# Tensor product of a graph network on one core: where TensorE reads a group's word, and where its loop body begins

## The chip, the core and the metric

One core of a Trainium2 chip runs the whole program. Its engines are TensorE (PE in the profile, its weight loads PEld, its sequencer PEq or PEldq), VectorE (DVE), ScalarE (ACT), GpSimd (POOL) and SyncE (SP, which starts DMAs). Each runs its own instruction stream, and they meet at semaphores. An engine's sequencer takes its stream in order: it handles registers, branches and waits itself and hands matmuls on to the array. The metric is the device time of one execution in microseconds.

## What is computed

Four layers of a graph network over 12,500 nodes and 400,000 edges, with a layer norm behind each. The change touches the last one, a tensor product over the edges. Cut to what matters (x are the node rows, sh1 the edge's direction, emb and edge_vec are inputs of the edge):

```
xs, xd = (x[edge_src], x[edge_dst])
s1 = concatenate([xs[:, :8], xd[:, :8]]); v1 = the other 24 columns of both as (16, 3)
w = _mlp(emb, fc1_w1, fc1_w2)                    # 10 -> 16 -> 512 weights of an edge
vdot1 = einsum('euk,ek->eu', v1, sh1) / SQRT3
s_t = a1 * (einsum('eu,euw->ew', s1, Wss) + einsum('eu,euw->ew', vdot1, Wvv))
v_t = a1 * (einsum('eu,euw->ew', s1, Wsv)[:, :, None] * sh1[:, None, :] + einsum('euk,euw->ewk', v1, Wvs))
w2 = _mlp(emb, fc2_w1, fc2_w2)                   # and the same once more on s_t, v_t: scal, gates, vecs
edge_out = concatenate([tanh(scal), vecs * tanh(gates)]) * norm
return segment_sum(edge_out, edge_dst)           # edges are sorted by edge_dst
```

## The kernel before

The edges are cut into 625 groups of 640 (5 tiles of 128). In this stage (`stage_tensor_product`) every engine runs one *turn* for each group, and a turn works on several groups at once, at different steps. SLOTS is 5 buffers, a loop body holds 15 turns (3 rounds of 5), and the body is run 41 times; the first and the last turns are written out beside it. The order within a turn is written out by hand in one function for each engine.

TensorE's turn is `pe_turn`. `there(i, j, off)` says whether the group `off` turns on exists, `at` names it. Before, it does in this order:

- `turn_words` (L2201, L2202): a wait and semaphore step, a register load of the group's word from SBUF and the arithmetic that cuts it up. The word tells the first block of own rows of the group two ahead (`first_ahead`) and how many visits that group (`n_ahead`) and the group three behind (`n`) need.
- `pe_contract` half 0 (matmuls L2537, 128 rows deep) and `pe_spread` half 1 (L2520, four matmuls on 32 rows each) of the group one behind,
- `pe_units` half 0 (L2509), `pe_turn_inputs` (transposes, L2547) of the next group, `pe_brackets` half 1 (L2495, four matmuls on 32 rows each),
- `pe_contract` half 1, `pe_turn_inputs` half 1,
- `pe_further_visits` for the group three behind: a test (L2572) whose body is jumped over where n is 1,
- `pe_return` (L2555), `pe_spread` half 0, `pe_units` half 1,
- `pe_own` (L2588 to L2592): the products with the own rows of the group two ahead, at an address made of `first_ahead`,
- `pe_brackets` half 0 of the next group: four matmuls in two pairs, each pair waiting (L2493) until VectorE has read the pair's two banks (`dve_second`, L2371),
- `pe_first_visit` (L2560), and `pe_own_further`: a test (L2599) whose body is jumped over where `n_ahead` is 1.

VectorE's turn runs, around the change: `dve_second` half 0 (L2371, a pair at a time), `dve_join` (L2347, needs `pe_own`), then as a new turn its own word, `dve_first` half 0 (L2363, a pair at a time, needs the pair of brackets), `dve_front` (L2354), `dve_first_visit` (L2425, needs `pe_first_visit`), `dve_second` half 1 (needs `pe_spread` half 1). `pe_spread` half 1 in turn needs, for each pair, `dve_first` half 0 of that pair, since both use the same banks. `pe_own` must wait for a DMA (`turned_in`) and for ScalarE's copies (`flipped`).

The loop jump of TensorE (L2732 in the profile) stands behind the 15th turn.

Of the kernel before, what the change touches and what calls it, by code (L numbers as in the profile page):

```python
# [14 lines left out]
ITERS = GROUPS // SLOTS  # L15
# [492 lines left out]
class Ranks:  # L508
# [7 lines left out]
    def at(self, i, n):  # L516
        return self.per * i + n
# [1641 lines left out]
def stage_tensor_product(nc, m, s):  # L2159
# [26 lines left out]
    def at(i, j, off):  # L2186
        return i + (j + off) // SLOTS, (j + off) % SLOTS

    def tile_of(j, k, off):
        return (k + (j + off) // SLOTS) % ROUNDS  # L2190

    def there(i, j, off):
        return not isinstance(i, int) or 0 <= SLOTS * i + j + off < GROUPS
# [13 lines left out]
    def turn_words(eng, i, j):  # L2207

        g = SLOTS * i + j
        if isinstance(i, int) and not 0 <= g < GROUPS:  # L2210
            first, n, _ = half_window_of(nc, eng, m, s, g + 2 if g < 0 else g - 3)
            return first, n, first, n
        return words_of(eng, g)
# [357 lines left out]
    def pe_further_visits(pe, i, j, n):  # L2571
        with pe.If(n > 1):  # L2572
            _, visits, further = half_window_of(nc, pe, m, s, SLOTS * i + j)
            pe.wait_ge(s["first_added"], ONE + SLOTS * i + j + 1)
            if not (isinstance(i, int) and SLOTS * i + j == GROUPS - 1):
                pe.wait_ge(s["summed_up"], ONE + SLOTS * i + j + 2)
            pe.sem_inc(s["going"], 1)
            with pe.Fori(1, visits) as k:
                pe.wait_ge(s["more_hot"], ONE + further + k)
                pe_product(sums_at(1), pieces(j), m["onehot_more"]).then_inc(s["summed"], 1)  # L2580
                pe.wait_ge(s["added"], ONE + further + k)
# [26 lines left out]

    def pe_turn(pe, i, j, k):

        if there(i, j, -3) or there(i, j, 2):
            _, n, first_ahead, n_ahead = turn_words(pe, i, j)
        if there(i, j, -1):
            pe_contract(pe, *at(i, j, -1), 0)
            pe_spread(pe, *at(i, j, -1), 1)
        if there(i, j, 0):
            pe_units(pe, i, j, 0)
        if there(i, j, 1):
            pe_turn_inputs(pe, *at(i, j, 1), 0)
        if there(i, j, 0):  # L2620
            pe_brackets(pe, i, j, 1)
        if there(i, j, -1):
            pe_contract(pe, *at(i, j, -1), 1)
        if there(i, j, 1):
            pe_turn_inputs(pe, *at(i, j, 1), 1)
        if there(i, j, -3):
            pe_further_visits(pe, *at(i, j, -3), n)
        if there(i, j, -1):
            pe_return(pe, *at(i, j, -1))
        if there(i, j, 0):  # L2630
            pe_spread(pe, i, j, 0)
            pe_units(pe, i, j, 1)
        if there(i, j, 2):
            pe_own(pe, *at(i, j, 2), tile_of(j, k, 2), first_ahead)
        if there(i, j, 1):
            pe_brackets(pe, *at(i, j, 1), 0)
        if there(i, j, -2):
            pe_first_visit(pe, *at(i, j, -2))
        if there(i, j, 2):
            pe_own_further(pe, *at(i, j, 2), n_ahead)  # L2640

    with nc.Block() as block:

        @block.sync
        def _(sp):
            sp_iteration(sp, 0, 0, False)
            for j in range(SLOTS):
                sp_group(sp, 0, j, 0, False)
            with sp.Fori(0, (ITERS - 2) // ROUNDS) as r:
                for i, k in rounds_of(r):  # L2650
                    for j in range(SLOTS):
                        sp_group(sp, i, j, k, True)
            for j in range(SLOTS):
                sp_group(sp, ITERS - 1, j, (ITERS - 1) % ROUNDS, True)
            sp_hot(sp, ITERS - 1, SLOTS - 1, True)
            sp.wait_ge(s["all_added"], ONE + 1)
            sp.dma_start(m["tmp"][HALF_P:P, :], m["acc"][0:HALF_P, NB * W:HALF_WINDOWS * W]).then_inc(s["halves_in"], 16)
            sp.dma_start(m["tmp"][0:HALF_P, W:NB * W], m["acc"][HALF_P:P, NB * W:(HALF_WINDOWS - 1) * W]).then_inc(s["halves_in"], 16)
            sp.wait_ge(s["finished"], ONE + 1)
            sp.dma_start(m["out"], m["x"][:, :]).then_inc(s["stored"], 16)  # L2660
            sp.wait_ge(s["stored"], 16)

        @block.gpsimd
        def _(pool):
            for j in range(3):
                pool_gather(pool, 0, j, 0, 0)
            for j in range(SLOTS):
                pool_turn(pool, 0, j, 0, 0)
            with pool.Fori(0, (ITERS - 2) // ROUNDS) as r:
                for i, k in rounds_of(r):  # L2670
                    for j in range(SLOTS):
                        pool_turn(pool, i, j, k, r if k else r + 1)
            for j in range(SLOTS):
                pool_turn(pool, ITERS - 1, j, (ITERS - 1) % ROUNDS, (ITERS - 1) // ROUNDS)
            for j in range(4):
                pool_pieces(pool, *at(ITERS, j, -4))

        @block.scalar
        def _(act):
            act_inputs(act, 0, 0)  # L2680
            act_turn(act, -1, SLOTS - 1)
            for j in range(SLOTS):
                act_turn(act, 0, j)
            with act.Fori(0, (ITERS - 2) // ROUNDS) as r:
                for i, _ in rounds_of(r):
                    for j in range(SLOTS):
                        act_turn(act, i, j)
            for j in range(SLOTS):
                act_turn(act, ITERS - 1, j)
            for j in range(3):  # L2690
                act_turn(act, ITERS, j)
            roots_act(nc, act, s, 1, m["root"][:, :])

        @block.vector
        def _(dve):
            nc.vector.memset(m["acc"][:, :], 0.0).then_inc(s["added_up"], 1)
            dve.wait_ge(s["added_up"], ONE + 1)
            _, n, _ = half_window_of(nc, dve, m, s, 0)
            dve_turned_further(dve, 0, 0, n)
            dve_join(dve, 0, 0)  # L2700
            dve_turn(dve, -1, SLOTS - 1, -1 % ROUNDS)
            for j in range(SLOTS):
                dve_turn(dve, 0, j, 0)
            with dve.Fori(0, (ITERS - 2) // ROUNDS) as r:
                for i, k in rounds_of(r):
                    for j in range(SLOTS):
                        dve_turn(dve, i, j, k)
            for j in range(SLOTS):
                dve_turn(dve, ITERS - 1, j, (ITERS - 1) % ROUNDS)
            for j in range(3):  # L2710
                dve_turn(dve, ITERS, j, ITERS % ROUNDS)
            _, n, further = half_window_of(nc, dve, m, s, GROUPS - 1)
            dve.wait_ge(s["first_gained"], ONE + GROUPS)
            dve.wait_ge(s["gained"], ONE + further + n - 1)
            link = Chain(dve, s["step"])
            cubed = lambda t: t[:, :].rearrange("p (b f) -> p b f", f=F)
            nc.vector.memset(m["tmp"][0:HALF_P, 0:W], 0.0).then_inc(s["all_added"], 1)
            link(nc.vector.tensor_tensor(m["x"][:, :], m["x"][:, :], m["acc"][:, 0:NB * W], ALU.add))
            dve.wait_ge(s["halves_in"], 32)
            link(nc.vector.tensor_tensor(m["x"][:, :], m["x"][:, :], m["tmp"][:, :], ALU.add))  # L2720
            layer_norm(nc, dve, link, s, 1, cubed(m["x"]), cubed(m["tmp"]), m["mean"][:, :], m["root"][:, :])
            nc.vector.nop().then_inc(s["finished"], 1)

        @block.tensor
        def _(pe):
            first, n, _ = half_window_of(nc, pe, m, s, 0)
            pe_own(pe, 0, 0, 0, first)
            pe_own_further(pe, 0, 0, n)
            pe_turn(pe, -1, SLOTS - 1, -1 % ROUNDS)
            for j in range(SLOTS):  # L2730
                pe_turn(pe, 0, j, 0)
            with pe.Fori(0, (ITERS - 2) // ROUNDS) as r:  # L2732
                for i, k in rounds_of(r):
                    for j in range(SLOTS):
                        pe_turn(pe, i, j, k)
            for j in range(SLOTS):
                pe_turn(pe, ITERS - 1, j, (ITERS - 1) % ROUNDS)
            for j in range(3):
                pe_turn(pe, ITERS, j, ITERS % ROUNDS)


def build(nc, d):
# [305 lines left out]
```

## Time and profile before

| | us |
|---|---|
| median of 3 runs | 25141.51 (25137.35 to 25158.99) |
| the profiled execution, its own time | 25140.86 |
| its span in the profile | 25139.1 |
| the tensor product's turns within it | about 18641 to 25086 |
| TensorE busy over the whole span | 59% |
| VectorE busy over the whole span | 61% |

The page's share of busy time covers all stages. The tensor product is the last quarter of the span, and there TensorE and VectorE are both close to full. All rows below are from that one execution; times in them count from the span's start.

### The profile page before, as it was taken

Reading aid. Unit: us, or ns where it says so; the run is one execution under the profiler, and the core shown is the slowest. Engines: PE = TensorE matmul, PEld = TensorE weight load, DVE = VectorE, ACT = ScalarE, POOL = GpSimd, SP = SyncE. Lnnn points to the kernel's source line nnn. Section 1 sums busy time; section 2 is a strip of 40 time slices with the busy share of each in tenths; the row PEclk is TensorE's granted clock in tenths of the full one; section 3 lists DMA queues with packets and bytes.
Section 4 is the critical chain, followed back from the end, with each engine's and each line's share of the span. In section 5 each row is a group of like instructions: output and inputs, shape, how many; then the busy total and the mean of one; then the engine's idle time right before and its main releaser. Section 6 shows DMA issues by size and latency. Waiting matters only on the chain. (4 is left out here: it accounts for less than half of the span.)

```text
span 25139.1 us, 445752 instructions
## 1 busy us (share of the span) xinstructions
PE 14765.1 (59%) x102440; PEld 8906.5 (35%) x102441; DVE 15355.5 (61%) x31597; ACT 5180.0 (21%) x13760; POOL 15775.7 (63%) x16798
## 2 busy tenths in 40 slices
PE   7555555576666669995100000000568888888888
PEld 5344444443434348892000000000523333333333
DVE  9766666656565654443111111599578888888888
ACT  4211111111111124441000000000023333333332
POOL 0377777677777764451677777776046666666665
PEclk9655555555555555555555555555579999999999
DMA  2466666633333335540211111122133333433333
GB/s 66 108 173 173 172 173 173 154 69 68 68 68 68 69 77 153 154 128 9 43 40 40 40 40 40 53 72 61 31 100 104 103 103 104 105 103 104 103 104 95
DMA packets 2469135, 2331.19 MB, mean 93 GB/s; under 512 B 1084287, under 2 KB 1990333, under 8 KB 2465922
## 3 DMA queue, kind: packets, MB, share of 16 engines
q1 hardware_dynamic: 1901630, 1900.27, 26.8%
q0 software_dynamic: 412544, 241.53, 6.6%
q10 hardware_dynamic: 153668, 172.93, 2.8%
q8 instruction: 717, 11.75, 0.2%
q14 instruction: 576, 4.72, 0.1%
HBM read 1765.30 MB, written 537.93 MB: 92 GB/s over the span
## 5 line engine op out<-in xcount | busy, mean ns | idle before, releaser
L768 POOL DMA_INDIRECT rows<-split_table,index x3125 | 2995.0, 958 | 1938.5 <-DMA index<-in_src 1007.0
L2255 POOL DMA_INDIRECT rows_x<-x_table,index x3125 | 2972.9, 951 | 1625.9 <-DMA index<-in_src 772.3
L1648 POOL DMA_INDIRECT rows_dram<-rows,place_now x3125 | 3026.2, 968 | 1487.9 <-issue 951.8
L884 POOL DMA_INDIRECT rows<-x_table,index x3125 | 3277.7, 1049 | 1021.1 <-issue 952.0
L1575 DVE TENSOR_REDUCE rows<-banks 128x108 f32<-128x324 f32 x1250 | 490.7, 434 | 3467.4 <-DMA rows_dram<-rows,place_now 3456.0
L1587 PE MATMUL banks<-row_pieces,hot_turned 128*128 x3125 | 393.7, 291 | 3604.0 <-DVE rows L1575 3542.1
L2371 DVE TENSOR_TENSOR second<-banks,h 128x768 f32<-128x768 f32 x2500 | 1944.7, 820 | 896.5 <-PE banks L2520 896.5
L2363 DVE TENSOR_TENSOR first<-banks,h 128x768 f32<-128x768 f32 x2500 | 1934.4, 815 | 155.7 <-issue 120.2
L576 PE MATMUL banks<-counts,low_turned 128*128 128x98 f32 x6250 | 1794.7, 435 | 79.3 <-ACT counts L564 49.5
L576 PEld LDWEIGHTS banks<-counts,low_turned 128*128 128x128 f32 x6250 | 1602.1, 315 | 204.1 <-issue 174.0
L2495 PE MATMUL banks<-u_turned,w_tensor 32*128 32x384 f32 (+1 forms) x10000 | 1529.6, 486 | 145.4 <-DVE second L2371 145.4
L1587 PEld LDWEIGHTS banks<-row_pieces,hot_turned 128*128 128x128 bf16 x3125 | 251.2, 134 | 3746.6 <-issue 3746.6
L976 PE MATMUL banks<-ident,rows 128*64 128x128 f32 x3125 | 734.1, 396 | 1305.4 <-DMA rows<-x_table,index 1301.2
L1065 PE MATMUL banks<-w,a 65*128 65x64 f32 x6250 | 1445.2, 418 | 90.4 <-DMA a<-a_dram 65.1
L1065 PEld LDWEIGHTS banks<-w,a 65*128 65x128 f32 x6250 | 1398.7, 332 | 172.5 <-issue 168.0
L2537 PE MATMUL banks<-second,w_second 128*32 128x384 f32 (+1 forms) x10000 | 1031.1, 482 | 495.9 <-issue 495.0
L2520 PE MATMUL banks<-units,unit_spread 32*128 32x384 f32 (+1 forms) x10000 | 1111.5, 516 | 0.3 <-DVE first L2363 0.3
L985 PE MATMUL banks<-flipped,w 64*64 64x512 f32 x1250 | 1104.5, 980 | 0.0
L2309 ACT COPY outputs<-banks 128x384 f32<-128x384 f32 x1250 | 531.4, 425 | 2711.3 <-PE banks L2537 2711.3
L1117 POOL TENSOR_TENSOR pieces<-rest,pieces 128x320 bf16<-128x320 f32 x625 | 479.8, 768 | 963.3 <-ACT pieces L1095 963.3
L947 ACT ACTIVATE lift<-banks,bias 64x640 f32<-64x640 f32 x625 | 492.6, 788 | 2808.8 <-PE banks L986 2790.3
L2509 PE MATMUL banks<-first,unit_sum 128*32 128x384 f32 (+1 forms) x10000 | 1063.5, 480 | 13.3 <-DVE first L2363 1.1
(480 smaller groups left out, 33435.6 us busy)
## 6 DMA issues: line engine op xcount, KB each, us to landing
h<-hidden_dram SPq DMA_DIRECT2D x1250, 320.0 KB
acc_moved<-dst_rows SPq DMA_DIRECT2D x625, 320.0 KB
src_row<-in_src_rows SPq DMA_DIRECT2D x625, 320.0 KB
hot_turned<-turned_dram SPq DMA_DIRECT2D x1250, 160.0 KB, 2.2
hot_dram<-onehot SPq DMA_DIRECT2D x625, 160.0 KB
turned_dram<-hot_turned SPq DMA_DIRECT2D x625, 160.0 KB
a_dram<-a ACTq DMA_DIRECT2D x625, 160.0 KB
a<-a_dram SPq DMA_DIRECT2D x625, 160.0 KB, 2.9
```

Of the source, the lines that this page charges most:

```text
L576: nc.tensor.matmul(self.look[:, wide], m["low_turned"][:, tile], m["counts"][:, wide], start=True, stop=False)
L768: nc.gpsimd.indirect_dma_start(out=m["rows"][j][:, t * SPLIT:(t + 1) * SPLIT], out_offset=None, in_=m["split_table"], in_offset=bass.Indir ...
L884: nc.gpsimd.indirect_dma_start(out=m["rows"][j][:, t * C2:t * C2 + F], out_offset=None, in_=m["x_table"], in_offset=bass.IndirectOffsetOnA ...
L985: nc.tensor.matmul(m["ps"][4][0:H, :], m["w"][0:C2, 0:H], flipped[:, 0:512], start=True, stop=True)
L1065: mm = nc.tensor.matmul(bank(j)[:, t * H:(t + 1) * H], m["a1"][j][0:W, t * P:(t + 1) * P], m["w"][0:W, 0:H], start=True, stop=True)
L1648: nc.gpsimd.indirect_dma_start(out=m["rows_dram"], out_offset=bass.IndirectOffsetOnAxis(ap=m["place_now"][j][:, t:t + 1], axis=0), in_=m[" ...
L2255: nc.gpsimd.indirect_dma_start(out=m["rows_x"][j][:, t * F:(t + 1) * F], out_offset=None, in_=m["x_table"], in_offset=bass.IndirectOffsetO ...
L2363: nc.vector.tensor_tensor(m["first"][2 * half + pair][:, :].rearrange("p (k e) -> p k e", k=2), bank_pair(4 + 2 * pair, width), rep(m["h1" ...
L2371: nc.vector.tensor_tensor(m["second"][pair][:, :].rearrange("p (k e) -> p k e", k=2)[:, :, columns(half)], bank_pair(4 + 2 * pair, width), ...
L2495: mm = nc.tensor.matmul(m["ps"][4 + chunk][:, 0:HALVES[half][1]], m["w_tensor"][rows, chunk * P:(chunk + 1) * P], m["u_turned"][j % 3][row ...
L2509: mm = nc.tensor.matmul(m["ps"][1][32 * chunk:32 * chunk + 32, 0:width], m["unit_sum"][:, :], m["first"][2 * half + chunk // 2][:, k * wid ...
L2520: mm = nc.tensor.matmul(m["ps"][4 + chunk][:, 0:HALVES[half][1]], m["unit_spread"][rows, :], m["units"][half][rows, :], start=True, stop=True)
```

## The change

The word is no longer read at the turn's head but behind `pe_units` half 1, in front of `pe_own`. The test of `pe_further_visits` moves with it, and so does the test of `pe_own_further`, which now follows `pe_own` directly. The turn ends there. `pe_brackets` half 0 and `pe_first_visit` become a function `pe_close`, which is called at the start of the next turn's part of the loop body with the indices of the turn before; so the loop jump now lies between `pe_own` (with its test) and `pe_brackets`, where it lay between `pe_own_further`'s test and the word. The order of the matmuls is the same as before but for the bodies of the two tests. Nothing is added or removed but calls of `pe_close`.

```diff
     def pe_turn(pe, i, j, k):
 
-        if there(i, j, -3) or there(i, j, 2):
-            _, n, first_ahead, n_ahead = turn_words(pe, i, j)
         if there(i, j, -1):
             pe_contract(pe, *at(i, j, -1), 0)
             pe_spread(pe, *at(i, j, -1), 1)
...
         if there(i, j, 1):
             pe_turn_inputs(pe, *at(i, j, 1), 1)
-        if there(i, j, -3):
-            pe_further_visits(pe, *at(i, j, -3), n)
         if there(i, j, -1):
             pe_return(pe, *at(i, j, -1))
         if there(i, j, 0):
             pe_spread(pe, i, j, 0)
             pe_units(pe, i, j, 1)
+        if there(i, j, -3) or there(i, j, 2):
+            _, n, first_ahead, n_ahead = turn_words(pe, i, j)
+        if there(i, j, -3):
+            pe_further_visits(pe, *at(i, j, -3), n)
         if there(i, j, 2):
             pe_own(pe, *at(i, j, 2), tile_of(j, k, 2), first_ahead)
+            pe_own_further(pe, *at(i, j, 2), n_ahead)
+
+    def pe_close(pe, i, j):
+
         if there(i, j, 1):
             pe_brackets(pe, *at(i, j, 1), 0)
         if there(i, j, -2):
             pe_first_visit(pe, *at(i, j, -2))
-        if there(i, j, 2):
-            pe_own_further(pe, *at(i, j, 2), n_ahead)
...
             with pe.Fori(0, (ITERS - 2) // ROUNDS) as r:
                 for i, k in rounds_of(r):
                     for j in range(SLOTS):
+                        pe_close(pe, *at(i, j, -1))
                         pe_turn(pe, i, j, k)
```

TensorE's stream in the middle of the loop body, one turn's end and the next one's head. ISA and REGISTER_ALU are steps of the sequencer, the rows behind a COMPARE_AND_BRANCH up to its UNCONDITIONAL_BRANCH (cut here) are the body that is jumped over. Before:

```order
L2509 MATMUL banks<-first,unit_sum 32x256 x4
L2588 ISA
L2592 ISA
L2592 MATMUL banks<-x_pieces,hot_turned 128x96 x5
L2495 MATMUL banks<-u_turned,w_tensor 128x384 x4
L2565 REGISTER_ALU
L2560 MATMUL banks<-pieces,hot_half 128x96 x5
L2599 REGISTER_ALU x2
L2599 COMPARE_AND_BRANCH
...
L2202 TENSOR_LOAD window
L2202 ISA x2
L2537 MATMUL banks<-second,w_second 32x384 x4
```

The same place of the changed kernel:

```order
L2509 MATMUL banks<-first,unit_sum 32x256 x4
...
L2202 TENSOR_LOAD window
L2202 ISA x2
L2572 REGISTER_ALU x2
L2572 COMPARE_AND_BRANCH
...
L2592 MATMUL banks<-x_pieces,hot_turned 128x96 x5
L2599 REGISTER_ALU x2
L2599 COMPARE_AND_BRANCH
...
L2495 MATMUL banks<-u_turned,w_tensor 128x384 x4
...
L2560 MATMUL banks<-pieces,hot_half 128x96 x5
L2537 MATMUL banks<-second,w_second 32x384 x4
```

The load of the word and both tests now stand between the units (L2509) and the brackets (L2495), and nothing of the sequencer's own stands between the first visit (L2560) and the contraction (L2537).

TensorE's stream at the end of the loop body. Before:

```order
L2560 MATMUL banks<-pieces,hot_half 128x96 x5
L2599 REGISTER_ALU x2
L2599 COMPARE_AND_BRANCH
...
L2732 REGISTER_ALU
L2732 COMPARE_AND_BRANCH
L2202 TENSOR_LOAD window
```

And now:

```order
L2592 MATMUL banks<-x_pieces,hot_turned 128x96 x5
L2599 REGISTER_ALU x2
L2599 COMPARE_AND_BRANCH
...
L2735 REGISTER_ALU
L2735 COMPARE_AND_BRANCH
L2495 MATMUL banks<-u_turned,w_tensor 128x384 x4
L2560 MATMUL banks<-pieces,hot_half 128x96 x5
```

The jump (L2732, L2735 in the changed file) stood behind the brackets and the first visit, and stands ahead of them now.

## Rows read from the trace of the kernel before

**Rows 1.** Busy time of the stage: us; PE, PEld, DVE, ACT, POOL (count); clock; DMA
```profile
18641.00:25086.00 6445.00, 5731.72 (x50797) 2373.80 (x50797) 5363.58 (x11492) 2038.55 (x6046) 4132.86 (x5414) 0.95 0.39 103
```

**Rows 2.** Chain that ended last, through one turn: start us, us, what
```profile
20026.04 0.85 PE banks L2537 x8
20026.89 0.65 PE banks L2520 x8
...
20031.47 0.87 PE banks L2520 x8
...
20033.46 1.69 PE banks L2495 x8
...
20035.47 0.54 issue
```

**Rows 3.** Waits of the stage: who waited for what, us in total, times, longest
```profile
PE banks L2537 <- issue: 484.4, 604, 4.9
```

**Rows 4.** TensorE's sequencer, one turn's head: count, ns min/median/max, first and last start
```profile
L2599 PEldq ALU_OP  x2: 36/36/36, 20034.5 to 20034.6; - x2
...
L2201 PEldq EVENT_SEMAPHORE  x1: 51/51/51, 20035.0 to 20035.0; - x1
...
L2202 PEldq TENSOR_LOAD <-window x1: 298/298/298, 20035.3 to 20035.3; - x1
...
L2534 PEldq EVENT_SEMAPHORE  x1: 51/51/51, 20035.9 to 20035.9; - x1
```

**Rows 5.** TensorE's sequencer, the further visits' test and the step behind it
```profile
L2572 PEldq ALU_OP  x2: 36/36/36, 20029.6 to 20029.7; - x2
...
L2553 PEldq EVENT_SEMAPHORE  x1: 51/51/51, 20030.2 to 20030.2; - x1
```

**Rows 6.** TensorE's sequencer, from behind the units to the brackets' wait
```profile
L2588 PEldq FUSED_REGOPS  x1: 37/37/37, 20031.6 to 20031.6; - x1
...
L2592 PEldq FUSED_REGOPS  x1: 94/94/94, 20031.8 to 20031.8; - x1
...
L2493 PEldq EVENT_SEMAPHORE  x1: 51/51/51, 20033.4 to 20033.4; - x1
```

**Rows 7.** Timeline of DVE ten microseconds earlier: start, us, line, op [idle before]
```profile
20024.10 0.65 DVE L2347 TENSOR_REDUCE u<-banks 128x160 f32<-128x480 f32 x1
20024.66 1.81 DVE L2363 TENSOR_TENSOR first<-banks,h 128x768 f32<-128x768 f32 x2
...
20027.57 0.69 DVE L2371 TENSOR_TENSOR second<-banks,h 128x512 f32<-128x512 f32 x1 [0.60 <-PE banks L2520]
```

**Rows 8.** The loaded word and the further visits' test in most of the turns
```profile
L2202 PEldq TENSOR_LOAD <-window x594: 296/302/321, 18704.2 to 25026.0; - x198
...
L2572 PEldq COMPARE_BRANCH  x593: 226/351/395, 18708.8 to 25020.7; - x198
```

**Rows 9.** The loop's jump, all of them, then the chain behind one
```profile
L2732 PEldq COMPARE_BRANCH  x40: 76/3620/4015, 18796.5 to 25035.7; - x40
...
20072.56 0.87 PE banks L2520 x8
...
20076.56 4.56 issue
...
20082.73 1.17 PE banks L2520 x8
```

**Rows 10.** Busy time around a turn's head where the clock fell, as in Rows 1
```profile
20032.80:20036.00 3.20, 2.41 (x22) 1.13 (x19) 3.20 (x5) 0.82 (x3) 1.66 (x4) 1.00 0.18 45
20036.00:20039.40 3.40, 3.39 (x24) 0.92 (x24) 1.66 (x5) 0.48 (x1) 2.67 (x3) 0.51 0.24 58
```

**Rows 11.** The chain: that turn's brackets and the next's, then brackets five turns apart
```profile
20044.81 1.69 PE banks L2495 x8
...
20132.39 1.78 PE banks L2495 x8
...
20183.68 1.78 PE banks L2495 x8
```

More of the change, by code:

```diff
@@ L2730, in _ @@
             for j in range(SLOTS):
+                pe_close(pe, *at(0, j, -1))
                 pe_turn(pe, 0, j, 0)
@@ L2734, in _ @@
                     for j in range(SLOTS):
+                        pe_close(pe, *at(i, j, -1))
                         pe_turn(pe, i, j, k)
             for j in range(SLOTS):
+                pe_close(pe, *at(ITERS - 1, j, -1))
                 pe_turn(pe, ITERS - 1, j, (ITERS - 1) % ROUNDS)
             for j in range(3):
+                pe_close(pe, *at(ITERS, j, -1))
                 pe_turn(pe, ITERS, j, ITERS % ROUNDS)
+            pe_close(pe, ITERS, 2)
 def build(nc, d):
```

## The prediction, made before the changed kernel ran

> **What bounds the kernel now.** I read the busy time by stage first. In the tensor product TensorE is busy for 5732 of 6445 us and VectorE for 5364 [rows 1], so neither has much room and a turn is set by a loop through both. Next the chain of waits of one turn [rows 2]: nearly all of it is matmuls, from the contraction at 26.04 (all such times here are 20000 plus the figure) to the next turn's at 36.01, which is 9.97 us, and one piece, the 0.54 us in front of that contraction, is "issue": the array has nothing and waits for no other engine. The list of waits has the sum: 484.4 us over 604 turns [rows 3]. That gap is what the change goes at, and the sequencer's own rows say what it is made of. From the brackets' second pair on the sequencer does the test of the own rows' further visits at 34.5, the word's semaphore step at 35.0, the load at 35.3, and reaches the contraction's wait at 35.9 [rows 4]. It is 0.9 us for the word (35.0 to 35.9) and 0.5 us for the test (34.5 to 35.0), while the array had the second pair and five small products to do. Elsewhere the sequencer has time: behind the units it makes the own rows' address from 31.6 to 31.9 and then stands until the brackets' wait is met at 33.4 [rows 6].
>
> **The change, step by step.** *At the head.* Word and test leave it. The contraction waits for nothing else (units and outputs were copied long before), so it would start as the first visit's products end, at 35.47 or a little sooner: 0.54 us earlier for TensorE.
>
> *Behind the units.* From 31.6 the sequencer now has to do: the word 0.9, the further visits' test 0.6 (29.6 to 30.2 [rows 5]), the own rows' address 0.3 [rows 6], their own test 0.5 [rows 4], and about 0.1 each to hand on the own products and to get from the brackets' wait to the first matmul (33.4 to 33.46 [rows 2, 6]). That is 2.5 us, so the brackets' first pair would start at about 34.1 and not at 33.46. 1.5 us of these steps (33.4 less 31.9) had been standing time; the cover is used up, with some 0.65 us over.
>
> *Who waits for that.* The brackets' second pair hangs on VectorE, which turns to the join at 34.10 (24.10 a turn earlier [rows 7]), just behind its last read of the banks; that pair starts at about 34.2 as before. Before, the pairs ran one behind the other, 1.69 us; the four matmuls of the spread, of the same size and also on 32 rows each, took 0.87 together [rows 2]. With both pairs ready at about the same time I take 0.87 to 0.95 for them: their end stays near 35.15, the first visit's at 35.47. So TensorE does reach the contraction 0.54 us early. But the first pair's result, which VectorE waits for, comes at about 35.0 to 35.1 (34.1 and a little over 0.9) in place of 34.4; VectorE began its first half at 34.66, straight behind the join [rows 7]. It begins some 0.4 us later now, and needs 1.81 us and then has its second product, which ends at about 36.9. The spread's second pair needs that one: it cannot start before 36.95, where the whole spread before started at 36.86 (26.89 and 9.97). Its end and with it the units half 0, which need all 128 rows, come at 37.5 to 37.6, within 0.1 us of before. VectorE itself is not late: its 0.60 us wait for the spread at 27.57 [rows 7] takes up the 0.4.
>
> So the 0.54 us at the head is given back, nearly all, one handover later. **A turn without disturbance keeps its length**: I take 0.0 us, between -0.13 and +0.13. The ends are those of the further visits' test, the one price that changes from turn to turn (its branch took 226 to 395 ns, 351 at the median [rows 8]), for an earlier or later start of the brackets goes straight into the loop. On some 600 turns that is -78 to +78 us.
>
> A page speaks against the move: by the Trainium skill, "DMA: Bandwidth & Descriptors", section on latency and other measured facts, a tensor_load has a floor of some 600 ns. Here 594 loads took 296 to 321 ns [rows 8], so the trace disagrees; by the page's price brackets would start 0.3 us later still, and the sum would end 180 us higher, at about 25160.
>
> *The loop's jump*, 40 times (one of them falls through at 76 ns), median 3.62 us [rows 9]. It lay behind the first visit: 4.56 us of gap, and the spread started 10.17 us behind the previous one (72.56 to 82.73). Now the jump starts at about 34.0 in a turn's time, so the brackets start at about 38.2 (0.2 for its registers, 3.6, and 0.4 to set up again), 6.8 us behind the spread at 31.47. They take 0.87, or twice that at the lower clock (the spread behind the jump took 1.17 against 0.65 [rows 2, 9]), VectorE's two products 1.81: the next spread's second pair starts 9.5 to 10.4 us behind the spread. Against 10.17 that is -0.7 to +0.2 each, -28 to +8 us in all; I take 0, since the lower clock is the usual case there.
>
> *The clock.* This is where I expect the gain. The mean granted clock of the stage is 0.95 [rows 1], and it does not only fall at the jumps. In the turn whose brackets start at 33.46 the clock is 1.00 up to the head and 0.51 for 3.4 us behind it [rows 10]; its contraction starts at 36.01 as usual, but the next brackets come at 44.81, 11.35 us on [rows 11], 1.38 more than a turn's 9.97. Five turns that hold one such fall take 51.29 us [rows 11], which is 4 x 9.97 and 11.35 to within 0.1; so about three turns of a body's 15 have one. What TensorE did before it fell: in the 3.2 us from the own products to the head it was busy for 2.41 us with 22 passes [rows 10], half of that the brackets in pairs on half of the array's rows, the rest small products and two gaps. The change brings the contraction, which uses all 128 rows, 0.54 us nearer to the units; the stretch of thin work is then 2.6 us in place of 3.2, though with gaps of about 0.6 and 0.2 us in it. I take it that these falls stop. It is a reading of one case and no row shows the new order, so the bounds are: none of them stop (0), or all (3 x 1.38 x 40 = 166 us).
>
> **Sum.** 25140.9 of the profiled execution (0.6 under the median of the runs) - 166 + 0 (turns) + 0 (jumps) = about 24975 us; with the turns' and jumps' bounds 24870 to 25060.
>
> **The rivals.**
> *The falls stay.* The idle time is only moved: 0.8 us of gaps in the same 3.2 us, which is what 3.20 less 2.41 was before [rows 10]. Then the time is 25141, between 25040 and 25225. For it: busy time alone would look the same. Against: the work of those 3.2 us grows by the contraction's first passes.
> *Slower: the sequencer is late at the brackets.* The place is the brackets' wait. Every 0.1 us beyond 34.1 there is 60 us; with the falls gone the kernel is slower by over 0.2% from 34.45 on, with the falls kept from 34.2 on. It would go so if the load of the word held until the units' products had left the array (31.47, 0.87 for the spread and two thirds of that for the units, which are 256 and not 384 columns wide: 32.9); then brackets start at 35.4 and the time is 25760; half of it, 25370. Against it speaks that the load at 35.3 began while the first visit was still at work until 35.47 [rows 2, 4]. For it: behind the units there are far more passes in the queue than there.
> *The tests are cheaper where they stand now.* If the further visits' test cost what the own rows' one does (0.5 in place of 0.6) and its branch the 226 ns of some turns, brackets start at 33.9 and each turn is 0.15 to 0.2 shorter: 24860. The Trainium skill, "Advanced Engine Details and Errata", section on control flow timing, has 108 ns for a compare and branch; no branch of these tests in the trace was under 200 ns, so I give this little.
> *More falls.* The wait in front of the own products may bring a fall of its own at another place of the turn. As many again would make it 25300.
>
> **How the numbers follow.** Forecast 0.57 (faster by over 0.2%, which is 50 us and about what a measurement of this kernel can tell from no change), falls stay 0.18 (same), sequencer late 0.15 (slower, but for a small part in which the falls make up for it), cheaper tests 0.05 (faster), more falls 0.05 (slower). Faster 0.64, same 0.18, slower 0.18. The range goes from 24870, the forecast's lower bound, to 25210, near the upper end of "falls stay"; it leaves out most of the last three rivals. The forecast's own is 24870 to 25060.
>
> **What the profile after would show.** Step 1: no "issue" wait in front of the contraction but for the jumps. Step 2: the sequencer's load at about 0.3 us behind the units' dispatch, the brackets' wait passed at about 34.0 in this turn's time, 2.5 us behind 31.6; VectorE waiting about 0.4 us for brackets in front of its first half. Step 3: turns of 9.9 to 10.1 us. Step 4: a mean clock of the stage of 0.97 or more and no turns of 11.3 us. The prediction is wrong if the clock stays at 0.95, or if brackets start later than 34.3 in a turn's time.

## The result, and the profile after

The changed kernel takes 24805.1 us (median of 4 runs, 24792.9 to 24818.5) where the kernel before takes 25140.7 beside it (4 runs, 25137.4 to 25159.0). The ratio is 0.9865, with a 95% interval of 0.9848 to 0.9882: 336 us faster, twice the 166 that were forecast, and below the range's lower end of 24870. The profiled execution has a span of 24798.6 us. Of all the runs told below one, a fourth of e9 (25806.8 us, at a mean granted clock of 0.583 where the other three have 0.654 to 0.656), ran in a slower state and is left out.

Busy time of the tensor product's stage in the profile after, with the columns of [rows 1] (us; PE, PEld, DVE, ACT, POOL, each with its count; clock; DMA share; GB/s):

```profile
18641.00:24740.00 6099.00, 5457.91 (x50693) 2390.53 (x50694) 5345.97 (x11465) 2025.05 (x6033) 4144.46 (x5408) 0.98 0.40 109
```

The mean clock is 0.98 where it was 0.95 in [rows 1], TensorE is busy for some 270 us less, VectorE for about as long as before.

The chain that ended last after the change, through one turn (start us, us, what; the answer to [rows 2]; times are again 20000 plus the figure where they are short):

```profile
20023.35 0.77 PE banks L2555 x5
20024.12 0.86 PE banks L2520 x8
20024.97 0.57 PE banks L2509 x8
20025.54 0.49 issue
20026.03 0.38 PE banks L2592 x5
20026.41 0.22 issue
20026.63 1.17 PE banks L2495 x8
20027.80 0.32 PE banks L2560 x5
20028.12 0.78 PE banks L2537 x8
20028.90 1.26 PE banks L2520 x8
```

The contraction (L2537) now stands straight behind the first visit (L2560): the 0.54 us of "issue" is gone from there. Two others have come, 0.49 in front of the own products (L2592) and 0.22 in front of the brackets (L2495). The brackets' two pairs take 1.17 and not 1.69. The waits of the stage (who waited for what, us in total, times, longest) have the sums; [rows 3]'s line is no longer among them:

```profile
PE banks L2495 <- issue: 282.9, 585, 4.6
PE banks L2592 <- issue: 269.6, 602, 0.8
...
DVE second L2371 <- PE banks L2520: 413.8, 645, 1.1
DVE first L2363 <- PE banks L2495: 266.8, 425, 5.2
```

VectorE now waits for the brackets in most turns; before, the last line read

```profile
DVE first L2363 <- PE banks L2495: 29.0, 37, 0.9
```

The sequencer's own rows of this turn say why VectorE waits (count, ns min/median/max, first and last start; six answers, one for each line of code):

```profile
L2507 PEldq EVENT_SEMAPHORE  x1: 51/51/51, 20023.8 to 20023.8; - x1
...
L2201 PEldq EVENT_SEMAPHORE  x1: 51/51/51, 20024.1 to 20024.1; - x1
...
L2202 PEldq TENSOR_LOAD <-window x1: 304/304/304, 20024.3 to 20024.3; - x1
...
L2572 PEldq COMPARE_BRANCH  x1: 361/361/361, 20025.2 to 20025.2; - x1
...
L2592 PEldq FUSED_REGOPS  x1: 89/89/89, 20025.9 to 20025.9; - x1
...
L2493 PEldq EVENT_SEMAPHORE  x1: 51/51/51, 20026.5 to 20026.5; - x1
```

From the word's step (L2201, 24.07 to two digits) to the brackets' wait (L2493, 26.52) the sequencer is at work without a break: 2.45 us. VectorE in the same turn (start, us, line, operation, idle before; as in [rows 7]):

```profile
20017.81 1.82 DVE L2363 TENSOR_TENSOR first<-banks,h 128x768 f32<-128x768 f32 x2 [0.19 <-PE banks L2495]
...
20022.50 1.29 DVE L2363 TENSOR_TENSOR first<-banks,h 128x512 f32<-128x512 f32 x2
...
20025.01 1.82 DVE L2371 TENSOR_TENSOR second<-banks,h 128x768 f32<-128x768 f32 x2 [0.63 <-PE banks L2520]
20026.74 0.65 DVE L2347 TENSOR_REDUCE u<-banks 128x160 f32<-128x480 f32 x1
20027.58 1.82 DVE L2363 TENSOR_TENSOR first<-banks,h 128x768 f32<-128x768 f32 x2 [0.19 <-PE banks L2495]
...
20029.81 1.28 DVE L2371 TENSOR_TENSOR second<-banks,h 128x512 f32<-128x512 f32 x2
```

From here the loop of the new kernel can be read off. VectorE works without idle time from its first half 0 (17.81) to the end of its first half 1 (22.50 and 1.29, 23.79): 5.98 us. The units' wait (L2507) is met then, and 0.28 later the sequencer begins the word. (Over 605 turns of either trace that wait is met 0.06 us behind the end of VectorE's first half 1, at the median and at both quartiles, before the change as after it.) Its run to the brackets' wait is 2.45, the brackets start 0.11 behind it (26.63), and 0.95 later VectorE has the first pair's result (27.58). 5.98 + 0.28 + 2.45 + 0.11 + 0.95 = 9.77 us, which is the distance from 17.81 to 27.58.

The jump at the head of the body, all of them and the chain behind one (the answer to [rows 9]):

```profile
L2735 PEldq COMPARE_BRANCH  x40: 76/3609/4115, 18777.6 to 24697.0; - x40
...
19991.44 3.83 issue
19995.26 1.77 PE banks L2495 x8
...
19998.99 1.17 PE banks L2520 x8
```

And brackets five turns apart in the chain (the answer to [rows 11]):

```profile
20016.85 1.17 PE banks L2495 x8
...
20065.84 1.17 PE banks L2495 x8
```

That is 48.99 us and not 51.29; none of the five holds a fall of the clock.

To split the 336 us I counted all 625 turns of both traces from one contraction's start to the next:

| | before | after | difference in all |
|---|---|---|---|
| turns with a fall of the clock and no jump | 116, of 11.35 us | none | 116 x 1.39 = 162 us |
| ordinary turns, mean | 9.957 us | 9.760 us | 624 x 0.197 = 123 us |
| turn with a jump and the next one, 40 times | 14.12 + 12.51 us | 14.23 + 10.62 us | 40 x 1.39 (over two ordinary turns) = 55 us |
| stage, first to last contraction | 6642.9 us | 6303.3 us | 339.6 us |

The three parts make the stage's 340 us. The falls gave what was forecast. The other two, forecast at nothing, gave the rest. Of the jumps' part much is clock too: the stage's time at the lower of the clock's two levels (granted 0.5) was 710 us in 158 stretches before and is 225 us in 40, one behind each jump. A turn with a jump and the next one hold 7.9 us of it in the mean before, 5.6 after. At the price of the other falls, 1.39 us for 3.4 us at the lower level, the 2.2 us between are some 0.9 of the 1.39 (an estimate).

### The profile page after: what moved, and what is told of

It is laid out like the page before. It is cut to its first block and busy times, and to the rows that moved or that the text cites. A ratio compares the mean times of both kernels' runs of the same rounds, so it can differ in the third digit from the quotient of the medians.

```text
span 24798.6 us, 445834 instructions
## 1 busy us (share of the span) xinstructions
PE 14500.5 (58%) x102440; PEld 8927.8 (36%) x102441; DVE 15351.3 (62%) x31597; ACT 5174.1 (21%) x13760; POOL 15792.5 (64%) x16798
## 5 line engine op out<-in xcount | busy, mean ns | idle before, releaser
L2495 PE MATMUL banks<-u_turned,w_tensor 32*128 32x384 f32 (+1 forms) x10000 | 1219.5, 489 | 296.8 <-issue 291.2
L2520 PE MATMUL banks<-units,unit_spread 32*128 32x384 f32 (+1 forms) x10000 | 1386.1, 486 | 6.9 <-DVE first L2363 2.9
L156 DVE TENSOR_REDUCE joined<-banks 128x33 f32<-128x99 f32 (+1 forms) x1250 | 390.5, 312 | 1074.3 <-PE banks L176 923.1
L926 DVE SCALAR_TENSOR_TENSOR a<-banks,bias,lift 64x640 f32<-64x640 f32 x625 | 546.0, 874 | 763.7 <-ACT lift L947 763.7
```

What stands on the lines that cost most here:

```text
L2495: mm = nc.tensor.matmul(m["ps"][4 + chunk][:, 0:HALVES[half][1]], m["w_tensor"][rows, chunk * P:(chunk + 1) * P], m["u_turned"][j % 3][row ...
L2520: mm = nc.tensor.matmul(m["ps"][4 + chunk][:, 0:HALVES[half][1]], m["unit_spread"][rows, :], m["units"][half][rows, :], start=True, stop=True)
```

## The experiments

Three questions stood open. **What sets the new turn**: my theory after the result was the loop above, through VectorE and the sequencer; the rival was the array's own sequence, as the prediction had it, with the shorter turn a matter of chance. **What the jump's new place is worth.** **What made the clock fall**: a gap of idle array behind thin work, that is matmuls on 32 rows or of few columns (the prediction), or the head's place in itself. Where a run stands alone, its time is one run; the kernel before took 25127 (runs e1, e4, e5, e6), 25135 (e2, e3, e8, e9), 25163 (e10) and 25150 us (e11, e12) beside them. Mean turns below are counted from contraction starts without the four turns around each jump, 464 in each trace; by that count the kernel before has 9.96 us in turns without a fall and 83 turns with one, the changed one 9.75 and none.

**e1: the jump in its old place.** The turn is the changed one; brackets and first visit close the body again.

```
             pe_own_further(pe, *at(i, j, 2), n_ahead)
+        pe_close(pe, i, j)
...
                     for j in range(SLOTS):
-                        pe_close(pe, *at(i, j, -1))
                         pe_turn(pe, i, j, k)
```

> The changed kernel's turn, but with the loop jump back behind the first visit (brackets and first visit end the turn again). It takes the part of the jump out of the gain. Theory A (the jump's place is worth what the traces of before and after show around it: the jump turn and the next one were 6.7 us over two ordinary turns before and 5.3 after): ordinary turns stay at 9.76, no long turns, and 40 jumps cost 1.4 us more each, about 24855. Theory B (the jump's place is worth nothing, the 1.4 us came from the word leaving the turn's head): about 24800.

Measured: 24744.4 us (4 runs, 24741.0 to 24748.9; ratio 0.9848, 0.9832 to 0.9865), less than either expectation. That is 61 us under the changed kernel; the kernel before was 14 us faster beside it, and in the traces the stage is 60 us shorter. The mean turn is 9.69 in place of 9.75, some 39 us in all, and the other 20 lie at the jumps.

The 39 need not be the jump's own. The sequencer's run from the word's step to the brackets' first matmul takes 2.45 us in the mean and not 2.51 (some 420 turns of each trace), for the same steps: the branch of the further visits' test is under 300 ns in 600 of 625 turns, in the changed kernel in 480. The 20 lie where the place changes the order: in the changed kernel the jump is one more step between the spread and the brackets, 6.4 us from the one's start to the other's and 2.5 here (medians of the 40 jumps).

So of the 55 us of the table nothing is the new place's doing. What is left is the word that no longer follows the jump at the head, and the shorter stretch at the lower clock (4.9 us in a jump's turn and the next, 7.9 before); no run parts the two. The array's idle time in front of the contraction is now 3.1 us for a jump, where it was 4.56 [rows 9]:

```profile
PE banks L2537 <- issue: 121.0, 39, 3.5
```

**e4: the word read twice**, the second time right behind the first.

```
             _, n, first_ahead, n_ahead = turn_words(pe, i, j)
+        if there(i, j, -3) or there(i, j, 2):
+            _, n, first_ahead, n_ahead = turn_words(pe, i, j)
```

> The changed kernel with the word read a second time in front of the own rows' products: 0.9 us more of the sequencer in front of the brackets, nothing else. Theory A (in the changed kernel the turn's loop runs through VectorE and then through the sequencer's steps between the units and the brackets): every turn is 0.9 us longer, 10.65 us, about 25340. Theory B (as predicted: the loop runs through the array, spread, units and return; the sequencer has room of a few tenths): turns of 9.8 to 10.2 us, 24830 to 25060.

Measured: 25217.4 us and a mean turn of 10.42, between the two expectations. The second word cost 0.69 us of the sequencer (the median of 605, from one word's last step to the next one's) and not the 0.9 I had put in. The branch of the test behind it is somewhat cheaper here than in the changed kernel, so that the run from the word's first step to the brackets' first matmul grew from 2.51 to 3.17 us in the mean, by 0.67. The mean turn grew from 9.75 to 10.42, by the same 0.67: what the sequencer's run gained, the turn gained. The waits of its stage:

```profile
PE banks L2592 <- issue: 662.4, 597, 1.3
PE banks L2495 <- issue: 288.7, 598, 4.5
...
DVE first L2363 <- PE banks L2495: 468.4, 598, 5.5
```

TensorE stands for 1.1 us of every turn in front of the own products, and no turn away from a jump holds a fall of the clock. In this run a gap at that place brought none.

**e5: no test for further visits** (the further visits of rows are left out, so part of the sum is not computed).

```
             _, n, first_ahead, n_ahead = turn_words(pe, i, j)
-        if there(i, j, -3):
-            pe_further_visits(pe, *at(i, j, -3), n)
```

> The changed kernel without the test of the further visits of a group (TensorE leaves these visits out): 0.5 us less of the sequencer in front of the brackets. Theory A: the turn shrinks by the 0.19 us that VectorE waits for brackets in the changed kernel and is then VectorE's own, 9.57 us, about 24690. Theory B: turns of 9.76 us as they were, about 24800.

Measured: 24683.0 us and a mean turn of 9.49, where the loop theory had 24690 and 9.57. The waits of its stage:

```profile
PE banks L2495 <- issue: 209.5, 47, 5.7
PE banks L2495 <- DVE second L2371: 145.4, 557, 0.6
...
DVE first L2363 <- PE banks L2495: 213.2, 40, 5.8
```

The brackets wait for the sequencer at little more than the jumps (47 times and not 585), and in 557 turns for VectorE, as before the change. VectorE waits for brackets 40 times and not 425. So the test is what brings the sequencer into the loop; without it the loop is the array's and VectorE's, at 9.49.

**e6: the word between the units and the inputs of the middle of the turn**, where the chain of waits shows the sequencer ahead of the array; the further visits' test back in front of the return.

```
             pe_units(pe, i, j, 0)
+        if there(i, j, -3) or there(i, j, 2):
+            _, n, first_ahead, n_ahead = turn_words(pe, i, j)
         if there(i, j, 1):
             pe_turn_inputs(pe, *at(i, j, 1), 0)
```

> The changed kernel with the word read between the units half 0 and the turned inputs, and the further visits' test back in front of the return: in both places the sequencer stands waiting in the trace of the changed kernel. In front of the brackets only the own rows' test is left. Theory A: the brackets' first pair hangs on VectorE's read of the banks again, VectorE runs without a wait for brackets, turns of 9.45 to 9.6 us, 24620 to 24710 if the clock holds; the pairs run one behind the other again, as before, and if that alone was what made the clock fall, about three turns of 15 are 1.4 us longer, 24780 to 24870. Theory B: about 24800.

Measured: 24746.4 us (4 runs, 24736.4 to 24751.2; ratio 0.9849, 0.9832 to 0.9865), and a mean turn of 9.74, about the changed kernel's. I had thought the place free. Its waits show that it is not:

```profile
PE banks L2495 <- DVE second L2371: 134.8, 565, 0.6
PE banks L2547 <- issue: 125.8, 572, 0.4
```

The inputs (L2547) wait 0.22 us for the sequencer in most turns. A sequencer that stands waiting (on L2493) does so behind the inputs' dispatch, not in front of it; I had read its idle time and not whose dispatch comes next.

**e3: the kernel before, with one line moved**: the own rows' test goes from the end of the turn to right behind the own products. The word stays at the head.

```
             pe_own(pe, *at(i, j, 2), tile_of(j, k, 2), first_ahead)
+            pe_own_further(pe, *at(i, j, 2), n_ahead)
...
-        if there(i, j, 2):
-            pe_own_further(pe, *at(i, j, 2), n_ahead)
```

> The kernel before with one edit: the test of the own rows' further visits stands directly behind the own products (in front of the brackets), where the sequencer of the kernel before stood waiting for 1.4 us. The word stays at the head, the jump in its old place. It takes 0.5 us of the sequencer's work out of the head and leaves 0.9. Theory F (the clock's falls in ordinary turns come of the gap at the head): the gap goes from 0.54 to 0.1 or less, the falls go with it, turns of 9.5 to 9.6 us, about 24750. Rival G (the falls come of the thin work, brackets in two pairs one behind the other with small products, gap or not): turns of 9.5 to 9.6 us but three in 15 longer by 1.4, about 24910.

Measured: 24675.8 us, no fall but at the jumps, a mean turn of 9.51. This one line is worth 459 us, more than the whole change. The chain at its head:

```profile
20031.46 0.32 PE banks L2560 x5
20031.77 0.10 issue
20031.88 0.85 PE banks L2537 x8
```

Without the test, 0.47 us, in front of it the word fits behind the brackets' second pair and the first visit, and 0.10 us of the 0.54 is left. The test, in its new place, runs in the time in which the sequencer stood waiting for the brackets. And the turn is shorter by 0.45, all of what the head lost (0.44): that part of the gap had been on the loop in full.

**e2: e3 with the jump in the changed kernel's place.**

```
     def pe_turn(pe, i, j, k):
 
+        if there(i, j, -3) or there(i, j, 2):
+            _, n, first_ahead, n_ahead = turn_words(pe, i, j)
...
-        if there(i, j, -3) or there(i, j, 2):
-            _, n, first_ahead, n_ahead = turn_words(pe, i, j)
-        if there(i, j, -3):
-            pe_further_visits(pe, *at(i, j, -3), n)
```

(against the changed kernel; the further visits' test goes back in front of the return)

> The same as e3_test_behind_own but with the loop jump in the changed kernel's place, in front of the brackets. Theory J (the jump's place is worth nothing: it stands in the turn's loop either way): within 30 us of e3_test_behind_own. Rival (the jump in front of the brackets gives VectorE nothing to do while it lasts): 40 to 80 us slower than e3_test_behind_own. The prediction's step would allow -28 to +8.

Measured: 24618.1 us, 58 less than e3. Neither expectation had a gain. The ordinary turn is the same (9.52 and 9.51); a jump costs 4.5 us over the ordinary turns here and 6.2 in e3, and 40 times 1.7 is 68. With the word at the head, the old place had jump and word one behind the other in front of the contraction; the new one parts them.

**e8: the word behind the contraction**, the rest as in e6.

```
         if there(i, j, -1):
             pe_contract(pe, *at(i, j, -1), 0)
+        if there(i, j, -3) or there(i, j, 2):
+            _, n, first_ahead, n_ahead = turn_words(pe, i, j)
+        if there(i, j, -1):
             pe_spread(pe, *at(i, j, -1), 1)
```

> The changed kernel with the word read between the contraction half 0 and the spread half 1, the further visits' test in front of the return as before, the own rows' test behind the own products: in e6_word_in_the_middle the sequencer stood for 1.0 us behind the contraction, while the word between units and turned inputs held the inputs up by 0.23 us. Theory A, refined (in e6 the loop runs through the array, and 0.23 us of it was the word): turns of 9.50 to 9.55 us, no falls, about 24610. Rival (VectorE or the pairs of brackets bound the turn at 9.76 in e6, the word was covered): 24745 as e6.

Measured: 24598.4 us (4 runs, 24595.1 to 24600.1; ratio 0.9786, 0.9770 to 0.9803), 536 us less than the kernel before and 207 less than the changed one: the best of all. Its mean turn is 9.49, and the waits of its stage have no "issue" in front of the contraction, the own products or the inputs; the one that is left is that of the 39 jumps:

```profile
PE banks L2495 <- DVE second L2371: 134.1, 565, 0.6
PE banks L2495 <- issue: 128.1, 39, 3.9
```

The word now runs while the array does the first visit and the contraction. The contraction is handed on while the brackets' second pair still runs, and the next dispatch is the spread's: in one turn the word runs from 23.92 to 24.86 and the spread starts at 25.50.

**e9: e8 with the jump in its old place** (the edit of e1).

> e8_word_behind_contraction with the loop jump back behind the first visit. Theory J: within 30 us of e8. Rival (as e1_old_jump was 55 us under the changed kernel: the old place is the better one for the jump itself): 40 to 80 us under e8.

Measured: 24623.7 us (3 runs, 24614.7 to 24628.7; ratio 0.9798, 0.9778 to 0.9817), some 25 more than e8, all of it at the jumps (the turn is 9.49 in both). The jump's new place is worth 25 here and 58 in e2, and costs 61 in the changed kernel, 20 of them at the jumps.

**e10 and e11: e3 with the word read twice, and three times, at the head**, to bring the gap back in front of the contraction without parting anything else.

```
             _, n, first_ahead, n_ahead = turn_words(pe, i, j)
+        if there(i, j, -3) or there(i, j, 2):
+            _, n, first_ahead, n_ahead = turn_words(pe, i, j)
```

(e11 has the two added lines twice)

> e3_test_behind_own (no falls, turns of 9.5) with the word read twice at the turn's head: some 0.75 us more of the sequencer there, as the second word added in e4_word_twice, so that the gap in front of the contraction is back, at about 0.8 us (0.54 before). In e4_word_twice the array stood idle for 1.1 us in front of the own products, in turns of 10.4 us, and the clock did not fall. Theory F, narrowed (it takes a gap at the head, right behind the brackets in pairs and the small products): turns of 10.2 us and falls again, about as many as before (116 in ordinary turns), about 25300. Rival (the place of the gap is nothing; falls came only of the kernel before's turn of 9.96 us): turns of 10.2 us, no falls, about 25130.

> As e10_gap_at_head but with the word read three times at the head: turns of about 11.0 us and a gap of some 1.5 us in front of the contraction. e10 had the gap and only 13 long turns where the kernel before has 116. Theory F, narrowed again (a gap at the head makes the clock fall, but which turns show it depends on the turn's length): many turns with a fall again, some 1.3 us longer each, total between 25750 and 26000. Rival (falls need the kernel before's turn of 9.96 us and nothing else): no long turns but behind jumps, about 25650.

Measured: 25208.6 us for e10. The turn grew by 0.72 to 10.23; 3 of the 464 turns away from the jumps hold a fall, and ten more next to a jump, neither some 116 in all nor none. For e11 26043.2 us: the turns without a fall take some 10.9, and 237 of 464 hold one or two. The waits in front of the contraction in e10 and in e11, and the stretch of e11's stage (columns as in [rows 1]):

```profile
PE banks L2537 <- issue: 639.7, 603, 5.1
```

```profile
PE banks L2537 <- issue: 932.0, 534, 5.8
...
18641.00:24600.00 5959.00, 4911.04 (x41496) 2004.02 (x41496) 4390.73 (x9389) 1668.15 (x4940) 3398.57 (x4447) 0.90 0.34 92
```

So without the gap, and with the same thin work, the falls away from the jumps are gone: none with about 0.1 us of it (e3), 83 turns of 464 with 0.54 (before). A gap of about 1.5 brings 237 (e11), but one of about 0.8 only 3 (e10), and this stands against the gap's length as the cause. The turn's length differs too, 9.5, 10.0, 10.9 and 10.2 in the same order; no run holds it fixed, so what makes the clock fall stays open.

**e12: e3 with an idle test behind the word at the head.**

```
+        if there(i, j, 2):
+            with pe.If(n_ahead > NB):
+                pe.sem_inc(s["going"], 1)
```

> As e3_test_behind_own with one idle branch of the sequencer behind the word at the head, 0.1 to 0.3 us: turns of 9.6 to 9.8 us with a gap of 0.1 to 0.35 us at the head. Theory F: few falls or none, for the gap is less than the 0.54 of before; 24730 to 24850. Rival (any gap behind the thin work is enough): about three turns of 15 with a fall, 24890 to 25010.

Measured: 24688.4 us, 13 more than e3 in one run each. Inconclusive: the bounds of the word make the condition false ahead of time, the trace shows no row of the test, and the gap at the head is 0.11, as good as e3's 0.10.

## Why the prediction was right and wrong

**The head: right.** No "issue" wait stands in front of the contraction any more.

**The sequencer's run: right in its parts.** From the word's step to the brackets' start it takes 2.56 us in the turn shown and 2.51 in the mean, where the prediction's parts make 2.5. VectorE waits for the brackets (0.19; 0.4 was said), and the first pair's result comes 0.95 behind their start, as taken. The rival "late at the brackets" was right that the sequencer bounds them, but the load did not hold for the units' products.

**"A turn without disturbance keeps its length" (0.0, between -0.13 and +0.13): wrong.** It is -0.20. This is the step that failed. The prediction closed its loop through the array; piece by piece, from the starts in the trace (here a spread starts with its first matmul's own start, 0.07 ahead of the chain's figure):

| piece of the loop, start to start | as predicted | measured |
|---|---|---|
| spread half 0 to brackets half 0 | 31.40 to 34.1: 2.70 | 24.04 to 26.63: 2.58 |
| brackets to the next spread's second pair | 34.1 to 36.95: 2.85 | 26.63 to 29.45: 2.83 |
| that pair to the units half 0 | some 0.6 | 29.45 to 30.09: 0.63 |
| units half 0 to the next spread half 0 | as before, 27.56 to 31.40: 3.84 | 30.09 to 33.82: 3.73 |
| sum | 9.99 | 9.77 |

Two of the four are off, by 0.12 and 0.11.

*The run's start.* I let the sequencer's run begin at 31.6, just behind the spread, as it had stood before, and so fixed it to the array. But what releases it is the units' wait on VectorE's first half 1, and the trace before had shown this: the wait is met 0.06 us behind that half's end there too. VectorE is earlier against the array now, its half ends 0.26 us ahead of the spread and not 0.07 (medians of 605 turns), and the word's step at 24.07 stands at the spread's start, not 0.2 behind it. The loop that bounds the new kernel is VectorE, sequencer, brackets, VectorE (9.77 by the profile after). e4 (0.67 of sequencer more, 0.67 of turn more) and e5 (without the test 9.49) show it.

*What the late head cost one step further on.* I looked for the head's gap at the head alone. In the kernel before, the sequencer was late for the units behind the contraction too. Its rows there, before and then after the change:

```profile
L2507 PEldq FUSED_REGOPS  x1: 42/42/42, 20027.5 to 20027.5; - x1
L2507 PEldq ALU_OP  x1: 32/32/32, 20027.6 to 20027.6; - x1
```

```profile
L2507 PEldq FUSED_REGOPS  x1: 42/42/42, 20029.5 to 20029.5; - x1
L2507 PEldq ALU_OP  x1: 32/32/32, 20029.6 to 20029.6; - x1
```

Before, the units started at 27.56 with the second of these steps still to come, and the inputs stood 0.89 us behind the units; after, the units start at 30.09, 0.48 behind that step, and the inputs follow in 0.78. That is the 0.11. The other traces agree (medians of ordinary turns): from the units to the inputs it is 0.89 us where word and test, or two words, stand at the head (before, e10), 0.81 with the word alone there (e3, e2), and 0.78 where the word is elsewhere and not in this piece (after, e1, e4, e5, e8).

**The jumps (0, between -28 and +8): wrong in size.** The region of a jump is 1.39 us shorter against ordinary turns. The piece that was worked out, from a spread to the next one's half 1, did come out: 9.9 us in the mean of the 40 jumps and 10.2 before, so -0.3 within -0.7 to +0.2. What was left out is what follows it, up to the next spread's half 0: 1.4 us at the lower clock there in place of 4.2. The prediction closed its sum at the first of these and let the lower clock last as long as before. e1 shows that the jump's new place is not the cause.

**The clock (-166): right in size, its reason open.** 162 us, and all falls outside the jumps are gone. The prediction said itself that no row shows its reason, and it took the upper of its two bounds; in part that was luck. The gap's end did end the falls in e3 as well, and a gap in front of the own products brought none (e4). That the amount of thin work decides was not shown: e3 has the brackets' pairs one behind the other and the first visit as before, and no falls; what it lacks is the gap. And e10 has a longer gap than the kernel before and 3 falls where that has 83.

**The rivals.** "The tests are cheaper" had the sign and about the size (24860), and the condition on the branch that it set: 226 ns at the median, where it was 351 [rows 8].

```profile
L2572 PEldq COMPARE_BRANCH  x607: 208/226/388, 18649.9 to 24759.1; - x152
```

But that is not what shortened the turn: the sequencer's run as a whole was as long as the prediction's parts made it, 2.51 us in the mean, and the turn shown above has the dear branch (361 ns) and is 9.77 us long all the same. "Falls stay" and "more falls" did not happen. Of the page that spoke against the move (the Trainium skill, "DMA: Bandwidth & Descriptors", latency facts, some 600 ns for a tensor_load), 604 loads of the word in the trace after have a median of 302 ns, as before; the trace disagrees and the sum was right to go by the row.

## What to carry to other kernels

A sequencer's gap in front of an engine is worth its full length only if its work finds a place where nothing is due next: e8 puts the same word where the next dispatch is over a microsecond off and gains 536 us, e6 puts it where the inputs are due and gains 380. Look for what makes the sequencer late before moving what stands nearest to the gap: the test in front of the word, moved alone (e3), gave 459 us. And when steps move from one engine's chain into another's, close the loop anew from the release that starts them; a start that is fixed to the old chain gives the old length back.

## What the runs showed that I had not expected

In the kernel before, the clock falls in turns with 0.54 us of idle array at the head; in e4, with 1.1 us of it in front of the own products, some 2 us ahead of the contraction, it does not. Idle time alone did not decide; whether the place or the turn's length did, no run shows.

The same steps of the sequencer take 2.32 us at some places of the unrolled body and 2.45 at others, in nearly every round: the branch of the further visits' test takes 226 ns in most and 361 in some, one step of the word comes 0.17 us later in others, and some have a register step more. The turns follow in the mean: those with the shorter run take 9.72 us, the others 9.80 (179 and 244 turns). In e1, with the code shifted by the jump's place, more turns have the short run. No run settles what decides it.
